# Scores of the second and third own-projection attentions: from full float32 matmuls to float32r matmuls on split operands, spread by SyncE transfers

## The reference, cut to what matters

```python
# layer 2 ("L2"): one key/value head shared by 16 query heads; c is the context
qh = (q @ w_q).reshape(B, L, 16, 8).transpose(0, 2, 1, 3)
k, v = (kvp[..., :8], kvp[..., 8:])                     # kvp = c @ w_kv
attn_score = jnp.einsum('bhid,bjd->bhij', qh, k) / np.sqrt(8)
out = jnp.einsum('bhij,bjd->bhid', jax.nn.softmax(attn_score, -1), v)
# layer 3 ("L3"): 16 heads of their own, key mask and causal mask of -1e9
scores = jnp.einsum('bhqd,bhkd->bhqk', q, k) / 8 ** 0.5
attn = jax.nn.softmax(jnp.where(m != 0, NEG, scores), axis=-1)
```

## Time and profile before

| | us |
|---|---|
| median of 3 runs | 1081.1 |
| lowest and highest | 1077.25, 1084.16 |
| span of the profiled execution | 1082.4 |
| first to last maximum of L2 (starts) | 472.8 to 655.5 |
| first to last maximum of L3 (starts) | 802.8 to 996.3 |

### The profile page before, as it was taken

The page is one execution under the profiler, slowest core; times in us unless marked ns, Lnnn a source line. Parts: engine busy times, 40 slices in busy tenths (PEclk is TensorE's granted clock), DMA queues, the critical chain, the costliest instruction groups (busy, mean ns, idle before and its releaser), DMA issues.

```text
span 1082.4 us, 29166 instructions
## 1 busy us (share of the span) xinstructions
PE 913.5 (84%) x9573; PEld 567.0 (52%) x9573; DVE 743.3 (69%) x2005; ACT 684.9 (63%) x1499; POOL 468.1 (43%) x999
## 2 busy tenths in 40 slices
PE   2898888995667856689999989878999899999898
PEld 2744444442345523334555544678864445454698
DVE  2667767765996979967888886337527776666344
ACT  3556666654875656667777764545676677775466
POOL 5422357671124523410144434668651258885200
PEclk9999989996667957799999999999999999999999
DMA  6977677636799997000000000866820001110011
GB/s 175 166 87 100 51 96 86 81 49 135 178 135 165 162 164 94 1 1 2 2 6 12 16 12 12 232 173 188 259 66 22 2 3 41 41 42 2 9 35 36
DMA packets 300444, 84.95 MB, mean 78 GB/s; under 512 B 211930, under 2 KB 287098, under 8 KB 300315
## 3 DMA queue, kind: packets, MB, share of 16 engines
q1 hardware_dynamic: 293962, 67.11, 38.3%
q0 software_dynamic: 5488, 15.88, 4.5%
q10 hardware_dynamic: 864, 0.27, 0.1%
HBM read 50.70 MB, written 35.51 MB: 80 GB/s over the span
## 4 chain that ended last, share of the span: by engine, by line
PE 61%; DVE 22%; issue 8%; POOL 3%; ACT 3%; DMA 2%; SPq 1%; DVEq 0%; ACTq 0%; POOLq 0%
PE bank L1284 16%; DVE nmax L1744 8%; PE bank L1316 7%; PE bank L1406 3%; PE bank L1298 3%; PE bank L1650 3%; PE bank L1642 3%; PE bank L1608 3%; PE bank L1596 3%; DVE small L1926 2%; PE bank L1287 2%; PE bank L1415 2%; PE bank L1274 2%; DVE stats L1679 1%; DVE q_one L1958 1%
## 5 line engine op out<-in xcount | busy, mean ns | idle before, releaser
L1744 DVE TENSOR_REDUCE nmax<-bank 128x8 f32<-128x1024 f32 x192 | 234.8, 1223 | 124.7 <-PE bank L1287 123.2
L960 ACT ACTIVATE probs_space<-bank 128x1024 f32<-128x1024 f32 x192 | 196.5, 1023 | 148.6 <-PE bank L1298 147.6
L1284 PE MATMUL bank<-q_one,k_all 32*128 32x512 f32 x768 | 218.1, 637 | 29.9 <-DVE nmax L1744 26.5
L1287 PE MATMUL bank<-k_one,q_all 32*128 32x512 f32 x768 | 217.4, 640 | 2.2 <-DVE nmax L1744 0.9
L1316 PEld LDWEIGHTS bank<-probs_space,vals 128*32 128x32 f32 x3072 | 73.0, 110 | 123.6 <-issue 122.8
L1316 PE MATMUL bank<-probs_space,vals 128*32 128x128 f32 x3072 | 125.6, 282 | 0.2 <-ACT probs_space L960 0.2
L1284 PEld LDWEIGHTS bank<-q_one,k_all 32*128 32x128 f32 x768 | 62.0, 185 | 59.2 <-issue 57.3
L647 POOL TENSOR_TENSOR var_b<-stats 128x8 f32<-128x8 f32 (+3 forms) x33 | 7.4, 223 | 175.2 <-DVE stats L1679 173.9
L722 POOL CAST nmax_parts<-nmax 128x16 bf16<-128x16 f32 x64 | 12.6, 196 | 160.9 <-DVE nmax L1744 145.5
L970 ACT ACTIVATE k_one<-k_all,one_head 128x512 f32<-128x512 f32 x96 | 68.9, 722 | 20.8 <-DVE k_all L1768 19.3
L1298 PE MATMUL bank<-nmax_one,ones_bf 12*128 12x512 bf16 x384 | 78.6, 381 | 0.0
(11 more groups left out here) (290 smaller groups left out, 2229.4 us busy)
## 6 DMA issues: line engine op xcount, KB each, us to landing
expert_rows<-zeros SPq DMA_DIRECT2D x8, 2322.0 KB, 38.4
context<-expert_w SPq DMA_DIRECT2D x31, 322.0 KB
k_one<-expert_w SPq DMA_DIRECT2D x15, 322.0 KB
late<-_L_ffn_down_weights_dram POOLq DMA_DIRECT2D x9, 512.0 KB, 5.4
late<-in_L_ffn_up_weights_dram POOLq DMA_DIRECT2D x9, 512.0 KB, 4.0
q_one<-expert_rows SPq DMA_DIRECT2D x46, 64.5 KB
q_scratch<-late SPq DMA_DIRECT2D x8, 256.0 KB
v_scratch<-moe_w SPq DMA_DIRECT2D x8, 256.0 KB
```

The source lines that it names most:

```text
L960: act.activation(probs[:, 2 * g:2 * g + 2, :, :].rearrange("k g i q -> k (g i q)"), bank_pair[1][:, :, :].rearrange("k g f -> k (g f)"), A ...
L1284: pe.matmul(bank[2 + s], group(k_all, u, 2 * g + s), group(q_one, u, 2 * g + s), start=not masked, stop=False)
L1287: m = pe.matmul(bank[s], group(q_all, v, 2 * f + s), group(k_one, v, 2 * f + s), start=not masked, stop=True)
L1744: dve.tensor_reduce(nmax[:, u % 2, 0, :].rearrange("q (g i) -> q g i", i=HG)[:, 2 * g:2 * g + 2, :], bank_pair[0][:, :, :].rearrange("q g ...
```

## The change

1. The scores of L2 and L3 are formed from operands declared float32r. Each projected quad is split into an upper half (the float with its low 12 bits cleared) and the rest, two DVE operations for keys and two for queries (`halves`). A 32-row group of the array now holds one head: its 8 channels times the four products upper x upper, upper x lower, lower x upper, lower x lower (`K_HALVES`, `Q_HALVES`).
2. SP spreads the halves into these rows: `rows_of_quad` issues transfers from SBUF to SBUF, each of 32 rows of 512 floats to every fourth partition. That is 20 transfers per quad in L2 (4 for keys, which all heads share, 16 for queries) and 32 in L3. Three row buffers per layer are used in turn; they lie in memory of `q_one`, `k_one`, `context` and `moe_w2`. `q_all` and `k_all` become single staging buffers: the next quad is copied there only when the last transfer of the quad before has landed.
3. `scores_of_heads` replaces the four matmuls of a half: in L2, 2 matmuls of 512 columns (tile u) and 8 of 128 columns (tile v, a head each); in L3, 16 of 128 columns.
4. ACT's zero-padded copies and DVE's two in L2 are gone. The score scale moves from the query copy to the exp.
5. Keys are projected at t = 4c - 7 and values at 4c - 4; the query copy stays at 4c - 5, the key copy moves to 4c - 6. DVE now takes part in the head iterations inside F1 (`VECTOR_BETWEEN`) and F2.
6. The three weights whose columns are reordered by head are loaded by four strided transfers each, nine more in all.

```diff
+UPPER_BITS = -4096
+Q_HALVES = (1, 0, 1, 0)
+K_HALVES = (1, 1, 0, 0)
+QUAD_BUFFERS = 3
...
+        ROW_BUFFERS = {"L2": (2, 0, 1), "L3": (0, 1, 3)}
...
-        TENSOR_BETWEEN = {12: range(-X_LEAD, -5), 13: (-5,), 14: (-4, -3)}
-        SCALAR_BETWEEN = {11: range(-X_LEAD, -6), 12: (-6, -5), 13: (-4, -3)}
+        TENSOR_BETWEEN = {11: range(-X_LEAD, -6), 12: (-6,), 13: (-5,), 14: (-4, -3)}
+        SCALAR_BETWEEN = {10: range(-X_LEAD, -6), 12: (-6, -5), 13: (-4, -3)}
+        VECTOR_BETWEEN = {13: range(-X_LEAD, -5), 14: (-5, -4, -3)}
...
+            def rows_of_quad(layer, c):
...
+                if c >= QUAD_BUFFERS:
+                    sp.wait_ge(S("t_s2"), 2 * QT * (quads + c - QUAD_BUFFERS + 1))
+                done = 4 * (own_quads + c)
+                for halves, buffers, of_row, n_slots in ((k_all, k_rows, K_HALVES, 1 if layer == "L2" else HG),
+                                                         (q_all, q_rows, Q_HALVES, HG)):
+                    for upper in (1, 0):
+                        done += 1
+                        sp.wait_ge(S("t_half"), done)
+                        for n in range(4):
+                            for i in range(n_slots):
+                                at = i if n_slots == HG else n
+                                if of_row[n] == upper:
+                                    sp.dma_start(rows_of(buffers, layer, c)[n:P:4, i, :].bitcast(F32),
+                                                 halves[HR * at:HR * at + HR, upper, :]).then_inc(S(name), 16)
...
             if "L2" in phases:
                 sp.wait_ge(S("L1_pv"), NT)
+                rows_of_quad("L2", 0)
+                sp.wait_ge(S("bit_yp"), 2 * NP)
+                sp.wait_ge(S("bit_hm"), 2 * NP)
+                for c in range(1, NQ):
+                    rows_of_quad("L2", c)
...
+                if "L3" in phases:
+                    sp.wait_ge(S("wT_out"), 2)
+                    sp.wait_ge(S("B_res"), NT_PART)
+                    rows_of_quad("L3", 0)
                 returned_rows(1, 0, 2)
+            if "L3" in phases:
+                sp.wait_ge(S("G_yo"), NS)
+                for c in range(1, NQ):
+                    rows_of_quad("L3", c)
...
+                def staging_free(c):
+
+                    if c > 0:
+                        name, landed = operands_in(layer, c - 1)
+                        act.wait_ge(S(name), landed)
...
-                                   ACT.Exp).then_inc(S("t_ex"), 1)
+                                   ACT.Exp, scale=SCORE_SCALE if own else 1.0).then_inc(S("t_ex"), 1)
...
+                def scores_of_heads(u, g, v, f):
...
+                    for s in range(2):
+                        if live(u) and shared_keys:
+                            pe.matmul(bank[2 + s], operand(k_rows, u, 2 * g + s, 0),
+                                      operand(q_rows, u, 2 * g + s, slice(0, HG)), start=not masked, stop=False)
+                    for i in range(HG):
+                        at = slice(i * P, i * P + P)
+                        for s in range(2):
+                            if live(u) and not shared_keys:
+                                pe.matmul(bank[2 + s][:, at], operand(k_rows, u, 2 * g + s, i),
+                                          operand(q_rows, u, 2 * g + s, i), start=not masked and i == 0, stop=False)
+                            if live(v):
+                                m = pe.matmul(bank[s][:, at], operand(q_rows, v, 2 * f + s, i),
+                                              operand(k_rows, v, 2 * f + s, 0 if shared_keys else i),
+                                              start=not masked and i == 0, stop=i == HG - 1)
...
                     if live(v):
-                        pe.wait_ge(S("t_qa"), quads + v // QT + 1)
-                        pe.wait_ge(S("t_k1"), HG * (quads + v // QT + 1))
+                        if own:
+                            name, landed = operands_in(layer, v // QT)
+                            pe.wait_ge(S(name), landed)
...
+                def halves(both, copied, c, done):
+
+                    done += 4 * (quads - NQ + c)
+                    dve.wait_ge(S(copied), quads + c + 1)
+                    dve.tensor_scalar(both[:, 1, :].bitcast(I32), both[:, 0, :].bitcast(I32), UPPER_BITS, None,
+                                      ALU.bitwise_and).then_inc(S("t_half"), 1)
+                    dve.wait_ge(S("t_half"), done + 1)
+                    dve.tensor_tensor(both[:, 0, :], both[:, 0, :], both[:, 1, :], ALU.subtract
+                                      ).then_inc(S("t_half"), 1)
...
-                    if layer not in SPLIT_BY_POOL and quad(t, 2) is not None:
-                        one_head_queries(quad(t, 2), 0)
-                    if layer not in SPLIT_BY_POOL and quad(t, 1) is not None:
-                        one_head_queries(quad(t, 1), 1)
+                    if own and quad(t, 6) is not None:
+                        halves(k_all, "t_kn", quad(t, 6), 0)
+                    if own and quad(t, 5) is not None:
+                        halves(q_all, "t_qa", quad(t, 5), 2)
```

More of the change, by code:

```diff
@@ L9 @@
 F32 = mybir.dt.float32
+F32R = mybir.dt.float32r
 BF16 = mybir.dt.bfloat16
@@ L401, in weights_in, with operands_in @@
                     (f"L0_v_slot_w{way - 2}", 16 * (NQ // 2 + n)))
+        N_ROW_DMAS = {"L2": HG * (1 + HG), "L3": HG * (HG + HG)}
+        def operands_in(layer, c):
+            n = c // QUAD_BUFFERS + 1
+            before = len(range(c % QUAD_BUFFERS, NQ, QUAD_BUFFERS)) * N_ROW_DMAS["L2"] if layer == "L3" else 0
+            return f"operands_in{c % QUAD_BUFFERS}", 16 * (before + n * N_ROW_DMAS[layer])
         def rows_out(slot):
@@ L999, in iteration @@
                                        quad_bank(c).rearrange("k (f d) -> k f d", d=DH), ACT.Copy).then_inc(S("t_ve"), 1)
-                    if quad(t, 4) is not None and (own or t > -3):
+                    if quad(t, 4) is not None and not own and t > -3:
                         one_head_keys(quad(t, 4), 0)
-                    if quad(t, 3) is not None and (own or t > -3):
+                    if quad(t, 3) is not None and not own and t > -3:
                         one_head_keys(quad(t, 3), 2)
@@ L1257, in pair_of_scores @@
                 def pair_of_scores(u, g, v, f):
                     if live(u):
[L1260 to L1261 removed]
+                        if not own:
+                            pe.wait_ge(S("t_q23"), 2 * (u // QT + 1))
+                            pe.wait_ge(S("t_q01"), 2 * (u // QT + 1))
                         past(pe, "t_ex", 2 * (tiles + u) + g)
                     if live(v):
[L1264 removed]
@@ L1385, in iteration @@
                     c = quad(t, 5)
[L1386 removed]
+                    if c is not None and not own and c > 0:
                         pe.wait_ge(S("t_qa"), quads + c + 1)
[L1388 to L1396 removed]
+                        pe.wait_ge(S("a_ctxT"), c + 1)
+                        for j in range(QT):
+                            m = pe.matmul(bank[5][:, j * P:(j + 1) * P], tile_of(contextT, QT * c + j), wk,
+                                          start=True, stop=True)
+                        m.then_inc(S("t_kp"), 1)
                     pair_of_scores(t, 1, t + 2, 0)
@@ L1433, in iteration @@
                         pe.matmul(quad_bank(c), wq, xnT_quad[:, :], start=True, stop=True).then_inc(S("t_qp"), 1)
-                    c = quad(t, 3)
+                    c = quad(t, 7)
                     if own and c is not None:
-                        pe.wait_ge(S("t_kn"), quads + c + 1)
+                        past(pe, "t_ve", own_quads + c)
+                        pe.matmul(quad_bank(c), wk, contextT[:, QT * P * c:QT * P * (c + 1)],
+                                  start=True, stop=True).then_inc(S("t_kp"), 1)
+                    c = quad(t, 4)
+                    if own and c is not None:
+                        pe.wait_ge(S("t_qa"), quads + c + 1)
                         for j in range(QT):
@@ L1895, in quantised_weights, with bit_ffn @@
                         link(dve.tensor_copy(ffn_sw[:, col:col + 1], quant_scale[:, i:i + 1]))
-            def bit_ffn(layer, gated, steps):
+            def bit_ffn(layer, gated, steps, next_iteration=None):
                 pairs = bit_pairs(layer)
                 for j in steps:
+                    for t in VECTOR_BETWEEN.get(j - 1, ()) if next_iteration is not None else ():
+                        next_iteration(t)
                     u, v = j + 4, j + 2
@@ L2007, in _ @@
                 quantised_weights(True, 5)
-                bit_ffn("F1", True, range(-4, NP))
+                iteration = attention("L2")
+                bit_ffn("F1", True, range(-4, NP), iteration)
             def slot_table(part, step):
@@ L2042, in _ @@
             if "L2" in phases:
-                iteration = attention("L2")
-                for t in range(iterations("L2").start, NT + 2):
+                for t in range(-2, NT + 2):
```

(1 more changed line is left out.)

129 lines of the change are left out of this document (75 added, 54 removed).

## The result

The changed kernel takes 1164.4 us (median; 1162.3 to 1171.7), the kernel before 1081.6 us on the same chip: ratio 1.077, 95% interval 1.072 to 1.082. The forecast was 1057 us.

A forecast was written before the change was run, and what follows sets the result against it. PE's scores alternating with DVE's maxima were taken to bound L2, and POOL beside PE L3's middle; 1082.4 less 12 in L2 and 13.5 in L3 gave 1056.9, forecast as 1057 us, range 1040 to 1092.

The forecast's parts named there:

- Score matmuls: PE in L2 and L3: a half's scores take 0.45 us instead of 1.02, saving 0.57.
- Rival A: The 128-column score matmuls cost full float32's 0.90 us a half: 1078 us, between 1070 and 1092; chance 0.22.
- Rival C: L2 and L3: granted clock falls; through both phases past 1150 us, in parts 1095 and up; chance 0.05.
- rival B: Transfers are late in L3: 1091 us at 0.7 us an issue, 1160 at 1.01; chance 0.13.
- Transfers: SP's queue: 0.47 us an issue, landing 2.0 after issue; 15.0 us a quad in L3, 9.4 in L2, hidden.
- 5 + 32p: Time of an L3 quad in us if an issue costs p; equals the 24.45 before at p = 0.61.
- Heads: Starts of L2 and L3: +6 us for L2; -1 for L3, quad 0's transfers fitting under F2's last slots.
- VectorE: Making the halves: AND 0.48 us, subtraction 0.6, two each a quad; net +1.2 a quad in L2, +2.2 in L3.
- rival E: Gain goes to small waits (semaphores between halves, POOL and DVE slowing each other): 1071 to 1082 us; chance 0.07.
- L2's steady part: About 6 quads of L2 with routing: DVE bounds at 22.5 us a quad against 24.2, -10 us.
- L3's middle: POOL limits iterations to 5.8 us against 6.1; 18 iterations give 0.3 each, -5.5 us.
- ScalarE's staging wait: ACT's staging copy waits for transfers, exps queued behind; ends where PE's own wait ends, so no price apart.

The follow-up runs named there:

- Fillers: Changed kernel plus two overwritten 128x512 bf16 matmuls of ones ahead of each half's scores in L2 and L3: 1134.8 us, ratio 1.046.
- old layout, one filler: Kernel before, L2 and L3 score operands as float32r, plus one overwritten matmul of ones a half: five executions 1036.3 to 1038.7 us, five 1053.8 to 1056.3.

## Why the prediction was wrong, step by step

- **Score matmuls.** 0.45 us a half was taken, 0.48 measured at full clock: right. The transposes of the earlier trace rows were the right row. The stacking within a row group that the Trainium skill's "TensorE: Matmul & The Clock Gate" (The mechanism, on packing small matmuls) would give, by the prediction's estimate 0.16 us a round, is not there: rounds are 0.11 to 0.14 us apart. (It is four matmuls to a row group in each half; the prediction says eight, but its sum is of four.) Rival A is out.
- **Rival C, the clock: the first of two steps that failed.** The sum took full clock throughout, and its fall had a chance of 0.05, because TensorE's busy share of 82% lay nearer the 87% of a stretch at 1.00 than the 60% of the earlier trace rows. In the stretches above it is 85% at 1.00, 91% at 0.63 and 88% at 0.79: the share does not tell the level, and it is itself larger at half clock because each matmul then takes longer. The clock measured 0.72 in L2 and 0.76 in L3. Fillers gave back 23.0 us of span, net of their own time: 14.6 in L2 and 5.2 in L3, 9.1 behind L3, and 5.1 lost at the head. The same skill page (its section on a second failure mode, psum-queue depth-cycling) describes a kernel whose clock goes back and forth where TensorE has short idle moments between groups of matmuls. That rule spoke against the change and was left out; the trace agrees in that such moments grew. In L2 TensorE waited 10.1 us in 18 waits for a maximum ahead of a half's scores before, and 15.5 us in 14 after. The one in the earlier trace rows is 0.40 us long; this one, still at full clock, is 1.15:

```profile
512.40 0.50 PE L1353 MATMUL bank<-q_rows,k_rows 32*128 32x512 f32 x2 [1.15 <-DVE nmax L1867]
```

That these moments are what lowers the clock is argued, not shown. The time named for C in parts, 1095 and up, holds, but it has no upper end, and rival B's part is in the measured time too.
- **Transfers: the second step, a mis-sized term.** 0.47 us an issue was taken from loads out of DRAM; 0.60 to 0.76 was measured. The formula was good: 5 + 32p is 27.4 us at p = 0.70, and quads of L3 took 28.0 to 29.0 between 900 and 1043 us. It put the break-even at 0.61; in L3 even the best group, at 0.64, was beyond that. Rival B, chance 0.13, is thus what happened in L3; halving the transfers gave back 17.1 us there.
- **Heads.** L2's: +6 forecast, +9.7 measured, 10.0 us of issues instead of 7.5. L3's: "fit under F2's last slots" was wrong. The keys of its quad 0 were issued from 818.25 and the queries until 839.40, the matmuls of F2 ended near 833, and TensorE then waited 8.32 us, and started at half clock. This and the clock are the +13.7 between the layers, where -1 was forecast.
- **VectorE.** 0.48 and 0.6 us forecast, 0.42 and 0.69 measured in L2: right. In L3 GpSimd stretches them (means of 0.70 and 1.14 us for the queries' two in the changed kernel, up to 1.39 and 1.91), which rival E named without a place. It stood at 0.07 and as at most 25 us; with both larger causes reduced it was worth up to 16.4 us.
- **L2's steady part.** 22.5 us a quad was forecast; the second quad, at full clock and before the routing, took 526.33 - 505.47 = 20.9, and those behind it, with clocks of 0.5 to 0.9, 24 to 30. The gain was there and was overlaid.
- **L3's middle.** GpSimd was forecast to bind at 5.8 us an iteration. It never did: at 7 us an iteration the transfers came first.
- **ScalarE's staging wait, "no price apart".** Five waits, 15.8 us, in L3. It is part of the transfers' cycle as assumed, and gets no term of its own.

The range ended at 1092 because C and the steeper part of B were given little; the 0.18 left out is B and C whole, so that the mild part of B, said to be inside, is counted nowhere. Both came true at once. Of the prediction's own signs, one record per matmul and the half's time came as named. TensorE idle for transfers once a head, ScalarE waiting for them in L3 and a clock under 1.00 in L2, its signs of B and C, came too. VectorE's idle time ahead of the maxima in L2, due to fall by half, went only from 31.7 to 28.0 us.

## What to carry to other kernels

When a change takes work from TensorE in a phase where it alternates with VectorE, do not judge the clock by the busy share: look for stretches of the same alternation at either level, and give a fall of the clock a real chance; a filler matmul in the idle moment is a cheap trial, and one in the wrong place cost 0.14 us here. Before packing operands into unused rows of a matmul, try the new type in the old layout: an empty row cost nothing here, and the transfers that fill it did. Weigh what exactness is lost by it. Price a DMA by a row with the same source and pattern, and write down the issue time at which the gain is gone; here it lay 0.14 us above the price taken, and the true one, about 0.70, beyond it.

## What the runs showed of the hardware

- A float32r matmul over 32 rows shows as one record where float32 shows two: 0.31 us from a half's four 512-column ones to the next group, against 1.02; with 128 columns and a new weight each, 0.11 to 0.14 us a round.
- 64 KB from 32 partitions of SBUF to every fourth partition: one issue in 0.60 to 0.76 us on SyncE's queue, against 0.47 for a load from DRAM of that size.
- Two fillers a half (0.59 us for the pair by the records) raised L2's clock from 0.72 to 0.94; a second set of score matmuls of about the half's own 0.48 us raised it only to 0.80. In L3 the two did about the same, 0.89 and 0.87 from 0.76. Why they differ in L2 stays open.
- VectorE's AND of 128x512 in SBUF went from 0.42 to as much as 1.83 us beside GpSimd's products and the subtraction from 0.69 to as much as 2.18.
- The same kernel (old layout, one filler) kept the clock in L2's last quad in some executions and lost it in others, 16 us apart, with the same work ahead of that point; what decides it was not found.
